# GIN neighbour sums on one Trainium2 core: node rows in two float32r parts, edge counts copied to float32r by VectorE

## The reference, cut to what matters

```python
agg = h + segment_sum(h[src], dst, num_segments=N)
z = relu(batch_norm(agg @ w1 + b1, g1, be1))
z = z @ w2 + b2
if g2 is not None:              # layers 0 and 1
    z = relu(batch_norm(z, g2, be2))
```

## Time and profile before

| | |
|---|---|
| time, median of 3 runs | 3797.47 us (3796.6 to 3804.4) |
| span of the profiled execution | 3802.4 us |
| PE busy / PEld busy | 82% / 47% of the span |
| DVE / ACT / POOL busy | 60% / 38% / 45% |
| GIN part (from 2951.9 us on) | about 850 us |
| DMA, mean | 171 GB/s |

### The profile page before, as it was taken

One profiled execution on the slowest core, in us unless ns is written; L12 is line 12 of the kernel. 1 busy time (PEld: TensorE's weight loads), 2 busy tenths in 40 slices (PEclk: granted clock), 3 DMA queues, 4 the chain that ended last, 5 costly groups with the idle time before them and its releaser, 6 DMA issues. The chain is left out here.

```text
span 3802.4 us, 61231 instructions
## 1 busy us (share of the span) xinstructions
PE 3102.2 (82%) x16127; PEld 1795.6 (47%) x16128; DVE 2280.6 (60%) x5544; ACT 1446.6 (38%) x3080; POOL 1719.9 (45%) x1731
## 2 busy tenths in 40 slices
PE   4547999989998689797689857769864899998996
PEld 2113444567776334496544336534332444544543
DVE  7556333558888989936799865689868202202104
ACT  0000222379998466530166642046544302202202
POOL 3777773036555765117777734767771000000000
PEclk9679999989999799888899978889985899999998
DMA  9997888468987454367511107934452321231321
GB/s 401 407 372 240 304 310 280 155 199 257 274 254 243 139 182 136 125 257 198 157 27 28 27 12 257 305 116 128 138 170 69 95 90 47 87 100 44 100 84 34
DMA packets 399994, 651.13 MB, mean 171 GB/s; under 512 B 129821, under 2 KB 274934, under 8 KB 392690
## 3 DMA queue, kind: packets, MB, share of 16 engines
q1 hardware_dynamic: 244441, 367.78, 30.4%
q0 software_dynamic: 72144, 145.54, 12.9%
q10 hardware_dynamic: 83213, 135.59, 9.6%
HBM read 468.36 MB, written 183.90 MB: 172 GB/s over the span
## 5 line engine op out<-in xcount | busy, mean ns | idle before, releaser
L1466 ACT ACTIVATE onehot<-iota,drel 128x128 f32<-128x128 f32 x1248 | 381.7, 388 | 685.4 <-PE ps L1169 345.4
L1229 PE MATMUL ps<-score_sb,shared_sb 128*128 128x512 f16 (+1 forms) x3150 | 625.2, 359 | 12.0 <-DVE shared_sb L2289 12.0
L1169 PE MATMUL ps<-shared_sb,onehot 128*128 128x264 f32 (+1 forms) x1600 | 552.6, 440 | 91.3 <-DVE accum L2257 86.3
L2257 DVE TENSOR_TENSOR accum<-accum,ps 128x264 f32 (+1 forms) x1248 | 527.7, 423 | 11.4 <-DVE accum L2257 4.5
L742 POOL DMA_INDIRECT t_w<-early_sb x391 | 416.1, 1064 | 165.1 <-issue 93.2
L759 POOL TENSOR_SCALAR onehot<-iota,carry_d 98x512 bf16<-98x512 f32 x28 | 43.6, 1561 | 942.8 <-PE ps L1246 802.0
L1229 PEld LDWEIGHTS ps<-score_sb,shared_sb 128*128 128x128 bf16 x3150 | 297.6, 98 | 335.3 <-issue 12.0
L1169 PEld LDWEIGHTS ps<-shared_sb,onehot 128*128 128x128 f32 x1600 | 256.2, 198 | 386.6 <-issue 245.5
L778 POOL DMA_INDIRECT shared_sb<-table,src_x x272 | 260.9, 959 | 116.1 <-issue 77.4
L778 POOL DMA_INDIRECT rows<-table,src_x x184 | 178.4, 970 | 179.9 <-DMA table<-score_sb 92.3
L825 POOL DMA_INDIRECT resid_sb<-table,src_x x224 | 211.6, 944 | 89.1 <-issue 57.3
(11 more groups left out here) (428 smaller groups left out, 5665.8 us busy)
## 6 DMA issues: line engine op xcount, KB each, us to landing
t_w<-onehot ACTq DMA_DIRECT2D x13, 6400.0 KB
score_sb<-t_adj SPq DMA_DIRECT2D x90, 640.0 KB, 3.9
accum<-t_hot SPq DMA_DIRECT2D x208, 256.0 KB
resid_sb<-t_w SPq DMA_DIRECT2D x13, 1664.0 KB
t_aside<-rows POOLq DMA_DIRECT2D x40, 512.0 KB
resid_sb<-t_w SPq DMA_DIRECT2D x13, 1536.0 KB
score_sb<-t_w SPq DMA_DIRECT2D x12, 1664.0 KB
shared_sb<-t_adj SPq DMA_DIRECT2D x30, 640.0 KB, 9.3
```

What stands on the lines that cost most here:

```text
L1169: pe.matmul(ps[:, RING[(HU * h + u) % len(RING)], 0:w], onehot[:, h % 2 * HU + u, :], around[g][place(g, i, h)][:, u, 0:w], start=True, st ...
L1229: mm = pe.matmul(ps[:, 2 * (i % 3) + f, 0:w], h_gin[:, t, m, f * P:(f + 1) * P], ring["gin"][:, at % HOLD, c, 0:w], start=(t == 0 and m == ...
L1466: last = act.activation(onehot[:, h % 2 * HU + u, :], iota[:, 0:P], ACT.Abs, bias=drel[:, bass.ds(step + u, 1)], scale=-1.0)
L2257: dve.tensor_tensor(to, to, bank.unsqueeze(1), ALU.add).then_inc(step_acc, 1)
```

## The change

- `split` for the node rows is replaced in the GIN layers: ACT copies the tile to float32r (`h_hi`), DVE subtracts it from the source into float32r (`h_lo`). The carried edges keep three bf16 parts.
- `block` issues 4 matmuls per tile and chunk (2 parts x 2 halves), with float32r on both sides.
- The counts no longer reach TensorE as f16. SP loads them into four landing buffers (`LAND`), DVE copies each block to one of four float32r buffers (`WORK`) in the new `widen(l, j)`, signalling `adj_whole`; TensorE waits for that. SP issues block j when block j - 4 has been copied; DVE copies block j when TensorE has finished block j - 4. The copies stand at fixed places in DVE's order.
- The buffers move: `z_gin` takes the place of `cols` behind layer 0's first product; the PSUM bank of a projection is given back when `h_lo` is made.

```diff
+            def counts_in(l, first, last):
+                for j in range(first, last):
+                    at = l * NC * GRP + j
+                    n, g = (j % 2, j // 2) if j < 2 * GRP else (j // GRP, j % GRP)
+                    if at >= LAND:
+                        sp.wait_ge(*count("adj_whole", at - LAND + 1))
+                    elif at == LAND - 1:
+                        sp.wait_ge(*count("l2r_tp", NT))
+                    w = 2 * P if SEQ[n] == NC - 1 else CW
+                    put(landing[at % LAND][:, :, 0:w], adj_view[SEQ[n], g][:, :, 0:w], adj_in[at % LAND])
...
-                    pe.wait_ge(adj_in[at % HOLD], kept_before[at % HOLD] + 16 * (at // HOLD + 1))
+                    pe.wait_ge(*count("adj_whole", at + 1))
...
-                        for m in range(3):
+                        for part in (h_hi, h_lo):
                             for f in range(DC):
-                                mm = pe.matmul(ps[:, 2 * (i % 3) + f, 0:w], h_gin[:, t, m, f * P:(f + 1) * P], ring["gin"][:, at % HOLD, c, 0:w],
-                                               start=(t == 0 and m == 0), stop=(i == 0 and t == NT - 1 and m == 2))
+                                mm = pe.matmul(ps[:, 2 * (i % 3) + f, 0:w], part[:, t, f * P:(f + 1) * P], whole_counts[at % WORK][:, c, 0:w],
+                                               start=(t == 0 and part is h_hi), stop=(i == 0 and t == NT - 1 and part is h_lo))
...
-                split(f"gin{l}", NT, (lambda t: resid[:, t, :]) if l == 0 else (lambda t: ps[:, 4 + t % 4, 0:D]),
...
+                    act.activation(h_hi[:, t, :], resid[:, t, :] if l == 0 else ps[:, 4 + t % 4, 0:D], ACT.Copy).then_inc(done(f"p0_gin{l}"), 1)
...
+            def widen(l, j):
+                at = l * NC * GRP + j
+                w = 2 * P if j < 2 * GRP and j % 2 == 0 else CW
+                dve.wait_ge(*counts_landed(at))
+                if at >= WORK:
+                    dve.wait_ge(adj_used, NC * GRP + at - WORK + 1)
+                dve.tensor_copy(whole_counts[at % WORK][:, :, 0:w], landing[at % LAND][:, :, 0:w]).then_inc(done("adj_whole"), 1)
...
+                if l == 0:
+                    for j in range(WORK):
+                        widen(0, j)
+                for t in range(NT):
+                    dve.wait_ge(*count(f"p0_gin{l}", t + 1))
+                    dve.tensor_tensor(h_lo[:, t, :], resid[:, t, :] if l == 0 else ps[:, 4 + t % 4, 0:D], h_hi[:, t, :], ALU.subtract
+                                      ).then_inc(done(f"split_gin{l}"), 1)
+                    if t >= GRP and t % GRP in (1, GRP - 1):
+                        widen(l, WORK + (t - GRP) // GRP * 2 + (t % GRP == GRP - 1))
+                for j in range(WORK + 2 * (GRP - 1), WORK + 2 * GRP):
+                    widen(l, j)
...
                 for i, n in enumerate(SEQ):
+                    for j in range(0, 0) if i == 1 else range(WORK + 2 * GRP if i == 0 else GRP * (i + 1) + WORK - 1,
+                                                              min(GRP * max(i + 2, 3) + WORK - 1, NC * GRP)):
+                        widen(l, j)
...
                 if l < 2:
+                    for j in range(WORK):
+                        widen(l + 1, j)
                     batch_norm(f"gin{l}b", accum_t, P, 2, f"L3_gnn_l{l}_g2", f"L3_gnn_l{l}_be2", lambda j, c: count(f"gin_mm2_{l}_ev", 2 * j + c + 1))
```

More of the change, by code:

```diff
@@ L28 @@
 HOLD, GRP = 8, 5
+LAND, WORK = 4, 4
 NG = NT // GRP
@@ L69 @@
 F16 = mybir.dt.float16
+F32R = mybir.dt.float32r
 ALU = mybir.AluOpType
@@ L83, in build, with over @@
     with ExitStack() as ctx:
+        place_of = {}
         def sb(name, shape, dt=F32):
-            return ctx.enter_context(nc.sbuf_tensor(name, shape, dt))
+            made = ctx.enter_context(nc.sbuf_tensor(name, shape, dt))
+            words = 1
+            for n in shape[1:]:
+                words *= n
+            place_of[name] = nc.sbuf_base - (words * (2 if dt in (BF16, F16) else 4) + 31) // 32 * 32
+            return made
+        def over(name, buf, first, shape):
+            return nc.alloc_sbuf_tensor_at(name, [P] + shape, F32R, offset=place_of[buf] + 4 * first)
         def sem(name):
@@ L240, in build @@
         key_gap = flat_a[:, 4224:4224 + 2 * L0H * P].rearrange("p (u e) -> p u e", u=2)
-        ring = {"gcn": shared_sb[:, 0:HOLD * GRP * CW // 2].bitcast(F16).rearrange("p (r c w) -> p r c w", r=HOLD, c=GRP),
-                "gin": score_sb[:, 0:HOLD * GRP * CW // 2].bitcast(F16).rearrange("p (r c w) -> p r c w", r=HOLD, c=GRP)}
+        ring = {"gcn": shared_sb[:, 0:HOLD * GRP * CW // 2].bitcast(F16).rearrange("p (r c w) -> p r c w", r=HOLD, c=GRP)}
+        landing = [buf.bitcast(F16).rearrange("p (c w) -> p c w", c=GRP) for buf in
+                   (early_sb[:, 0:GRP * CW // 2], score_sb[:, 11520:11520 + GRP * CW // 2], flat_o[:, 512:512 + GRP * CW // 2],
+                    shared_sb[:, 8960:8960 + GRP * CW // 2])]
+        whole_counts = [over(f"counts_r{r}", buf, first, [GRP, CW]) for r, (buf, first) in
+                        enumerate((("shared_sb", 6400), ("score_sb", 6400), ("score_sb", 8960), ("reset_f", 0)))]
         ends_at = onehot[:, :, :].rearrange("p u w -> p (u w)").bitcast(BF16)[:, 0:2 * CW].rearrange("p (r w) -> p r w", r=2)
@@ L258, in build @@
         crest_gcn = flat_pk[0:EQ, 2240:2240 + 64]
[L259 to L262, removed]
+        h_hi, h_lo = over("h_hi", "shared_sb", 0, [NT, D]), over("h_lo", "score_sb", 0, [NT, D])
+        z_gin = shared_sb[:, 0:2 * NP].rearrange("p (c n) -> p c n", c=2)
+        c_gin = shared_sb[:, 10240:10240 + 2 * EQ].rearrange("p (c w) -> p c w", c=2)
+        cb_gin = score_sb[0:EQ, 12800:12800 + 3 * D // 2].bitcast(BF16).rearrange("p (m d) -> p m d", m=3)
+        crest_gin = score_sb[0:EQ, 13184:13184 + D]
         ps = ctx.enter_context(nc.psum_tensor("ps", [P, 8, 512], F32))
@@ L315, in build @@
         parts = [(f"{c}{n}", 1 if c else (5 if n == "gcn" else NT)) for n in dense for c in ("", "c")]
+        in_three = [(n, c) for n, c in parts if n == "gcn" or n[0] == "c"]
         products = [("gcn", NT), ("gat1", NT), ("gatw", DC * NC), ("gat2", NT), ("gin_last", NT)]
@@ L323, in build @@
                   [("bnsc_" + n, c) for n, c in norms],
-                  by_layer("al_t", 8, 4, 4), by_layer("scan_f", 8, 4, 4), by_layer("scan_r", 8, 4, 4), by_layer("peak_t", 4, 4, 4),
+                  by_layer("al_t", 8, 4, 4) + [("adj_whole", 3 * NC * GRP)], by_layer("scan_f", 8, 4, 4), by_layer("scan_r", 8, 4, 4), by_layer("peak_t", 4, 4, 4),
                   [(f"peak_ev{k}", 1) for k in (1, 2)], by_layer("ends", 2, 2, 2), by_layer("carried", 2, 2, 2), by_layer("carry_t", 2, 2, 2),
@@ L331, in build @@
                   [("weighted1", 2), ("self_w1", 1), ("weighted2", 2), ("self_w2", 1)], [("diag_clear", 1), ("apart", S // QU), ("gaps", 3 * (S // HU))], [("x1_back", 16), ("x2_back", 16)], [("quad_sum", QUADS), ("own_mm", NT), ("adj_turned", BLOCKS * PAIRS)], [("same_act", QUADS), ("adj_staged", BLOCKS * PAIRS)], [("w_summed", QUADS), ("own_sum", NT)], [("step_mask", EB), ("te", 1), ("adj_rows", 1), ("adj_ev", 1), ("keys", 2), ("pre", 1), ("attr_split", 1)], [("te_ps", 3), ("adj_tp", 1), ("steps_ps", 2), ("steps_ev", 1), ("early_one", 1)],
-                  [("p0_" + n, c) for n, c in parts], [("rest_" + n, c) for n, c in parts],
-                  [("p1_" + n, c) for n, c in parts], [("split_" + n, c) for n, c in parts],
+                  [("p0_" + n, c) for n, c in parts], [("rest_" + n, c) for n, c in in_three],
+                  [("p1_" + n, c) for n, c in in_three], [("split_" + n, c) for n, c in parts],
                   [("carry_ev_" + n, 1) for n in dense], [("carry_tp_" + n, 1) for n in dense[1:]],
@@ L382, in adjacency_kept, with counts_landed @@
                 engine.wait_ge(adj_kept[n], 16 * PAIRS)
+        def counts_landed(at):
+            before = len(range(at % LAND, NC * GRP, HOLD)) + at // LAND + 1
+            return adj_in[at % LAND], kept_before[at % LAND] + 16 * before
         def first_lap(i):
@@ L625, in _, with ring_in @@
             adj_view = t_adj.rearrange("(n p g c w) o -> n g p c (w o)", n=NC, p=P, g=NT // GRP, c=GRP)
-            def ring_in(into, lap, first, last):
+            def ring_in(first, last):
                 for j in range(first, last):
[L630 to L633, removed]
+                    n, g = j // GRP, j % GRP
+                    if j >= HOLD:
+                        sp.wait_ge(adj_used, j - HOLD + 1)
                     w = 2 * P if SEQ[n] == NC - 1 else CW
-                    put(ring[into][:, at % HOLD, :, 0:w], adj_view[SEQ[n], g][:, :, 0:w], adj_in[at % HOLD])
+                    put(ring["gcn"][:, j % HOLD, :, 0:w], adj_view[SEQ[n], g][:, :, 0:w], adj_in[j % HOLD])
+            def counts_in(l, first, last):
[8 more added lines that the diff above has]
+                    put(landing[at % LAND][:, :, 0:w], adj_view[SEQ[n], g][:, :, 0:w], adj_in[at % LAND])
```

(4 more changed lines are left out.)

29 lines of the change are left out of this document (14 added, 15 removed).

## The result

| | time, us | runs |
|---|---|---|
| before, beside the changed kernel | 3797.03 (3794.89 to 3804.4) | 4 |
| changed | 3637.93 (3625.65 to 3642.44) | 4 |
| ratio | 0.9576, 95% interval [0.9553, 0.9598] | |
| changed, measured again beside the kernel before | 0.9555 [0.9537, 0.9573], median 3631.99 | 5 and 9 |

The change takes 159 us off the medians, 162 between the two profiled spans (3802.4 and 3640.7). The forecast was 187 off, 3611 us; the range of 3598 to 3670 holds the measured time, the narrower band of 3600 to 3630 does not. The profiled execution of the changed kernel took 3642.44 us.

A forecast was written before the change was run, and what follows sets the result against it. TensorE's matmul stream in the GIN sums was taken as the bound, matmuls times spacing. Terms -191.7 + 0.3 + 3.4 + 1.3 gave about -187 us, so 3611 us from the 3797.47 median; range 3598 to 3670.

The forecast's parts named there:

- narrower band of 3600 to 3630: Whole kernel: the forecast as worked out, in us, given a chance of 0.50.
- step 1: Wide matmuls of the GIN sums: 2700 at 0.217 us become 1800 at 0.219, gain 191.7 us.
- rivals B: L1229's stream: two passes for every float32r matmul, 3999 us; chance 0.13 with its worse form.
- its worse form: Same stream: four passes per float32r matmul, as a full f32 call, some 4790 us; within the 0.13.
- rival A: Narrow float32r matmuls are charged four passes, wide ones one: 3651 us; chance 0.25.
- stalls: A mixture with stalls, put together with DVE becoming the stage's pace: mostly 3630 to 3720 us; joint chance 0.12.
- steps 2 and 3: Narrow matmuls at 0.125 us: +0.3 us in layer 0; with projections, +3.4 us for layers 1 and 2.
- step 4: Count copies on DVE within the layers: 1.5 us wide, 0.8 narrow, hidden behind TensorE's stream.
- rival C: DVE's copies become the stage's pace: 3700 us at 5 us a copy; chance 0.12 including a mixture with stalls.
- step 5: Four copies ahead of layer 0 are not hidden: TensorE starts later, +1.3 us.
- steps 6 and 7: Splits at 2 operations per tile instead of 4, and loads with four blocks outstanding instead of eight: 0 each.

The follow-up runs named there:

- The experiment with one column: Changed kernel with wide matmuls of layers 1 and 2 reading one column of the counts 512 times instead of 512 columns: 3617.07 us.

## Why the prediction came out as it did

**What bounds the kernel: right.** The time of the stage is the number of TensorE's matmuls times their spacing. Dropping a third of them gave the gain, and undoing everything but that (two f16 parts) gave it too.

**Wide matmuls (step 1): mechanism right, size off.** One pass, as taken; rivals B and its worse form are out. The term was sized with 0.219 us, read off f32 streams, and measured 0.2316: 1800 x 0.2316 = 417 us. Read in the same way, the 2700 of before cost 0.2158 each, 583 us, so the gain is 166 us and not 192. These 26 us are nearly all of the 28 by which the forecast gain (187) exceeds the measured one (159). The sentence that missed is the one that let the f32 stream of 256 columns stand for float32r, "array time plus nothing". At 0.216 us for 256 columns that stream spends 0.84 ns on a column, nearly twice float32r's 0.445; it could show that a load hides, but not how fast fresh four-byte columns can come. The experiment with one column shows that this is the cause. Two-byte columns at 0.2158 have no such cost.

The prediction named a sign of being wrong, a wide spacing over 0.23 us, and 0.2316 is over it. The time still fell in the range because its upper part had been left for rival A and stalls, and none of them came: that the range held is in part luck.

**Narrow matmuls (steps 2 and 3): the bound right, both sizes off.** They are held up by the load, as taken: 0.112 us at the full clock, against 0.125 (of the two streams behind that figure, the one at 0.135 ran at a mean granted clock of 0.82, so it was not a warm one). Rival A is out: at 152 columns 0.072 us is reached with a short load, and the widths 256 and 384 show no step either. The price before was misread too. The 0.081 us is a mean over a phase that starts at the lower clock; in the kernel before, the first narrow block of 30 takes 3.75 us and each later one 1.97, 0.066 us apiece. Four at 0.112 cost about what six at 0.066 did: in layers 1 and 2 the change costs next to nothing (1.31 against 1.30 us a tile, forecast +0.08), but dropping a third of the narrow ones saves nothing either. In layer 0 the phase of chunks 6 and 0 went from 44.5 to 37.5 us, where about 35 was forecast: its wide blocks from 32.9 to 24.4, its narrow ones from 11.6 to 13.1, +1.5 us against +0.3. The first 20 narrow ones ran at 0.213 us, at the granted clock of 0.50 behind a wait of 12 us, which the forecast priced at the full clock's rate.

**Copies (step 4): right**, 1.5 us and hidden, with room: even doubled they leave the stream alone, so rival C is out. A narrow one took 0.95 and not 0.8.

**The late start (step 5): right.** The wait went from 11.07 to 12.19 us, +1.1 against +1.3 forecast, although four copies took 4.5 us there: the kernel before had spent part of that time waiting for ACT.

**Splits and loads (steps 6 and 7): right**: within the sums no wait of TensorE names them.

By layer, from the first matmul of the sum to the first behind the last fold, layer 0 went from 215.0 to 161.9 us. From the first projection to the start of the last folds, layer 1 went from 234.8 to 180.6 us (first projection at 3233.23 before, 3182.28 after) and layer 2 from 236.1 to 179.2 (3507.95 and 3403.46). That is 53, 54 and 57 us, 164 in all, of which the later start of the sums and small shifts around them take back 2. The 3 us that layer 2 gives more than layer 1 are not the change's: its first four projections took 5.22 us in layer 1 and 6.53 in layer 2 before, 6.35 and 5.00 after, at mean granted clocks of 0.67, 0.53, 0.52 and 0.66. With the wide term put right, the sum of the prediction comes to -161 us, within 2 us of both the medians and the spans; the smaller terms are off by 1 to 3 us each and cancel in part.

## What to carry to other kernels

Where TensorE's stream is the bound, count matmuls first, then ask what one column of each operand costs to fetch: fewer parts paid here in either format, but two-byte parts paid 41 us more and needed no copies. If a number is cut into parts, the type that the other operand already has (here f16 counts, so f16 parts) should be tried before a wider one. A stream of another type shows only what it has in common with the new one; write down which rate it can't show.

## What the runs showed of the hardware that I had not expected

- A float32r matmul steps at 0.445 ns a column (512, 384 and 256 columns) at a granted clock of 1.00, where f16 steps at 0.417. With a step-zero moving side it runs at 0.218 us for 512 columns, close to f16's 0.216.
- Its weight load, 188 ns for 128 columns, is hidden behind 512 columns and even behind 256 at a spacing of 0.118 us. At 152 columns it is not: the spacing is 0.112 us, 0.072 when only 64 columns are loaded, and 0.066 with f16.
- Neither 134 GB/s of DMA into SBUF, nor VectorE's copies, nor zeros for data move the spacing of 0.2316 us by more than 0.001 us.
